# Attention matmuls of two sequences in one stretch, every second slot, and another order of the beginning

## The reference

```python
# layer 0: conditioned layer norm
out = (x - mean) * rsqrt(var + 1e-5) * weight + bias
out = (out + tanh(cond @ lin_w.T + lin_b)[:, None, :]) * weight + bias
# layer 1: conditioned transformer block, each gamma, beta, alpha = (cond @ w.T)[:, None, :]
h = gamma_a * rmsnorm(x) + beta_a
q, k, v = heads(h @ W_q.T), heads(h @ W_k.T), heads(h @ W_v.T)     # 16 heads of 16
x = x + alpha_a * (softmax(0.25 * q @ k.T) @ v) @ W_o.T            # per sequence, 64 x 64
h = gamma_f * rmsnorm(x) + beta_f
x = x + alpha_f * ((silu(h @ gate_w.T) * (h @ hidden_w.T)) @ out_w.T + out_b)   # 1024 hidden
```

## Time and profile before

| | |
|---|---|
| median of 3 runs | 1042.36 us (1040.92 to 1042.98) |
| the profiled execution | 1042.48 us, span 1040.7 us |
| busy TensorE / VectorE / ScalarE / GpSimd | 989.9 / 682.4 / 619.2 / 567.3 us |
| share of the span | 95 / 66 / 59 / 55 % |
| mean granted clock of TensorE | 0.988 of 2.4 GHz |
| first scores (L376) | 32.15 us |
| last small product of the attention (L398, slot 130) | 987.5 us |

### The profile page before, as it was taken

The page is one execution under the profiler, slowest core; times in us unless marked ns, Lnnn a source line. Parts: engine busy times, 40 slices in busy tenths (PEclk is TensorE's granted clock), DMA queues, the critical chain, the costliest instruction groups (busy, mean ns, idle before and its releaser), DMA issues.

```text
span 1040.7 us, 28677 instructions
## 1 busy us (share of the span) xinstructions
PE 989.9 (95%) x11292; PEld 920.9 (88%) x11292; DVE 682.4 (66%) x1310; ACT 619.2 (59%) x1733; POOL 567.3 (55%) x531
## 2 busy tenths in 40 slices
PE   5777999999999999999999999999999999999997
PEld 4665998999999999999999999999999899999897
DVE  4677666666666666676666667666676766666554
ACT  3456565666566566656656665665666566666432
POOL 3477646566474656647465564746656474443320
PEclk9889999999999999999999999999999999999999
DMA  6010001000100000000000000001000000000000
GB/s 203 2 62 21 2 11 33 11 23 12 32 12 12 32 12 22 12 30 15 12 32 12 22 12 17 27 12 32 12 22 12 12 13 12 12 12 13 11 12 21
DMA packets 20884, 23.37 MB, mean 22 GB/s; under 512 B 1168, under 2 KB 20240, under 8 KB 20752
## 3 DMA queue, kind: packets, MB, share of 16 engines
q1 hardware_dynamic: 20752, 21.54, 6.4%
HBM read 13.15 MB, written 8.39 MB: 21 GB/s over the span
## 4 chain that ended last, share of the span: by engine, by line
PE 68%; DVE 9%; ACT 7%; issue 7%; ACTq 0%; POOLq 0%; POOL 0%; DVEq 0%
PE psum L263 13%; PE psum L265 12%; PE psum L264 12%; PE psum L387 5%; PE psum L453 4%; PE psum L452 4%; PE psum L376 4%; PE psum L451 4%; PE psum L398 3%; ACT probs L778 3%; PE psum L293 1%; PE psum L301 1%; PE psum L306 1%; DVE merge L510 1%; DVE least L547 1%
## 5 line engine op out<-in xcount | busy, mean ns | idle before, releaser
L263 PE MATMUL psum<-xf_hi,ffn_hi 128*128 128x256 f32 x1024 | 287.6, 281 | 3.9 <-DVE normed_f L589 1.6
L264 PE MATMUL psum<-xf_lo,ffn_hi 128*128 128x256 f32 x1024 | 286.2, 280 | 0.0
L265 PE MATMUL psum<-xf_hi,ffn_lo 128*128 128x256 f32 x1024 | 285.6, 279 | 0.0
L778 ACT ACTIVATE probs<-psum,least 128x64 f32<-128x64 f32 x928 | 202.4, 330 | 50.1 <-DVE least L547 26.7
L612 DVE SCALAR_TENSOR_TENSOR late<-tanh,psum 128x512 f32<-128x512 f32 x128 | 88.1, 688 | 207.1 <-ACT tanh L801 206.8
L944 POOL TENSOR_TENSOR probs<-probs,inv_sum 128x512 f32<-128x512 f32 x128 | 141.9, 1109 | 128.3 <-DVE inv_sum L565 127.6
L807 ACT ACTIVATE prod_hi<-late 128x512 fp32r<-128x512 f32 x128 | 80.8, 631 | 210.4 <-DVE late L620 210.4
L263 PEld LDWEIGHTS psum<-xf_hi,ffn_hi 128*128 128x128 f32 x1024 | 192.5, 188 | 5.1 <-issue 3.8
L264 PEld LDWEIGHTS psum<-xf_lo,ffn_hi 128*128 128x128 f32 x1024 | 192.7, 188 | 0.0
L265 PEld LDWEIGHTS psum<-xf_hi,ffn_lo 128*128 128x128 f32 x1024 | 192.6, 188 | 0.0
L626 DVE TENSOR_TENSOR prod_lo<-late,prod_hi 128x512 fp32r<-128x512 f32 x128 | 88.7, 693 | 89.3 <-ACT prod_hi L807 89.3
(11 more groups left out here) (100 smaller groups left out, 2264.0 us busy)
## 6 DMA issues: line engine op xcount, KB each, us to landing
xin<-x_dram SPq DMA_DIRECT2D x16, 512.0 KB, 3.8
out_t_dram<-x_res SPq DMA_DIRECT2D x32, 256.0 KB, 2.1
w_raw<-attn_w_dram SPq DMA_DIRECT2D x1, 1024.0 KB, 7.6
x_res<-gate_w_dram SPq DMA_DIRECT2D x1, 1024.0 KB, 10.4
late<-hidden_w_dram SPq DMA_DIRECT2D x1, 1024.0 KB, 12.1
x_res<-out_w_dram SPq DMA_DIRECT2D x1, 1024.0 KB, 5.6
k_heads<-mod_w_dram SPq DMA_DIRECT2D x1, 448.0 KB, 5.4
ident<-identity_dram SPq DMA_DIRECT2D x1, 64.0 KB, 3.3
```

Source lines behind the costliest of these rows:

```text
L263: pe.matmul(out, stat_hi, mov_hi, start=first, stop=False)
L264: pe.matmul(out, stat_hi, mov_lo, start=False, stop=False)
L265: return pe.matmul(out, stat_lo, mov_hi, start=False, stop=last)
L778: op = act.activation(probs[g % 2][:, h * SEQ:(h + 1) * SEQ], scores[:, h // 2, h % 2], ACT.Exp, bias=least[g % 2][:, h:h + 1], scale=-1.0)
```

## The change

The slots of attention are paired. TensorE has nothing of attention in odd slots. In even slots it turns sequence s-2 (into bank 0, as before) and s-1 (into the last 128 columns of banks 3 to 6, `odd_turned`), multiplies s-4 and s-3 with the values, and makes the scores of s and s+1. VectorE finds both minima in the even slot, behind both scores. The exponentials, row sums and reciprocals of the odd sequence stay in the odd slot; GpSimd normalises both in the odd slot, the even one first and the odd one last. ScalarE copies both turned tiles in the even slot, the odd one only when both new minima are found. `centre` is left to even sequences. The mean-square matmuls (j = 1) go behind the projection. In odd slots `invert_sums` goes ahead of `activate`; the statistics of the tokens go behind `product`. In the beginning the loads have another order and are split in halves, weights of the FFN are split from slot -4 on, and queries and values of part 0 have another bank, so that keys, queries and norms follow each other in another order.

```diff
@@ constants
-SPLIT_AT = -1
+SPLITS = {-4: (0, 1), -3: (2,), -2: (3,), 0: (4,), 1: (5,), 2: (6,), 3: (7,), 4: (8,), 5: (9,), 6: (10,), 7: (11,)}
+OUT_W_AT = -1
@@ PSUM
-        scores = psum[:, 3:7, 0:2 * SEQ].rearrange("p r (a k) -> p r a k", k=SEQ)
-        attended_t = psum[:, 3:7, 2 * SEQ:4 * SEQ].rearrange("p s (h t) -> p h s t", h=2)
+        scores = [psum[:, 3:7, i * P:(i + 1) * P].rearrange("p r (a k) -> p r a k", k=SEQ) for i in range(2)]
+        attended_t = psum[:, 3:7, 2 * P:3 * P].rearrange("p s (h t) -> p h s t", h=2)
+        odd_turned = psum[:, 3:7, 3 * P:4 * P]
@@
         def wide(g):
-            return g < FFN_AT
+            return g < FFN_AT and g % 2 == 0
+        def norm_step(s):
+            return 3 if s == -2 else 2 if s == -1 else s % PSEQ
+        def proj_bank(w, m):
+            return y_bank if m == 0 and w in (WQ, WV) else work
@@ SyncE, loads
-            load_x(0)
+            sp.dma_start(cond_sb[0:COND, 0:BATCH], cond_t).then_inc(mod_loaded, 16)
+            load_mod(SHIFT, A_BETA, mod_loaded)
+            load_half(0)
             sp.dma_start(ident[:], identity).then_inc(loaded, 16)
...
-            sp.dma_start(cond_sb[0:COND, 0:BATCH], cond_t).then_inc(mod_loaded, 16)
-            sp.dma_start(mod_stage[:, 0:7 * D].rearrange("p (w d) -> p w d", d=D),
-                         mod_w.rearrange("w c d -> c w d")).then_inc(mod_loaded, 16)
+            load_half(1)
+            load_mod(A_BETA, F_ALPHA + 1, rest_loaded)
@@ TensorE
             def score_banks_free(s):
                 if is_seq(s - 1):
                     pe.wait_ge(scores_read, s)
-                if s % PSEQ == 3 and is_part(s // PSEQ - 1):
-                    pe.wait_ge(att_lo_made, s // PSEQ)
+                if is_seq(s - 3):
+                    pe.wait_ge(probsT_out, s - 2)
+                if s % PSEQ == 0 and is_part(s // PSEQ - 2):
+                    pe.wait_ge(att_lo_made, s // PSEQ - 1)
@@ turn_probs
                 pe.wait_ge(probs_made, g + 1)
-                if g >= 1:
-                    pe.wait_ge(probsT_out, g)
-                if g + 2 - FFN_AT >= 1:
+                if g % 2 == 0 and g + 2 - FFN_AT >= 1:
                     pe.wait_ge(act_made, g + 2 - FFN_AT)
@@ TensorE, the slot
-                if is_seq(s - 2):
-                    turn_probs(s - 2)
-                score_banks_free(s)
-                if is_seq(s - 3):
-                    times_values(s - 3)
-                if is_seq(s):
-                    score(s)
-                norm_bank_free(s)
+                if s % 2 == 0:
+                    if is_seq(s - 2):
+                        turn_probs(s - 2)
+                    score_banks_free(s)
+                    if is_seq(s - 1):
+                        turn_probs(s - 1)
+                    for g in (s - 4, s - 3):
+                        if is_seq(g):
+                            times_values(g)
+                    for g in (s, s + 1):
+                        if is_seq(g):
+                            score(g)
+                if norm_step(s) != 1 or s < 0:
+                    norm_bank_free(s)
...
+                if s == 0:
+                    values(0)
                 if j == 0 and is_part(grp + 1):
                     keys(grp + 1)
...
+                if norm_step(s) == 1 and is_group(grp) and s >= 0:
+                    norm_bank_free(s)
+                    mean_squares(grp)
                 if is_step(f):
                     gate(f)
@@ VectorE, the slot
-                if is_seq(s):
-                    find_least(s)
-                    if wide(s):
-                        centre(s)
+                if s % 2 == 0:
+                    for g in (s, s + 1):
+                        if is_seq(g):
+                            find_least(g)
+                            if wide(g):
+                                centre(g)
...
-                if grp % 2 == 0 and 2 <= (grp + 4) // 2 < NBLK:
-                    token_stats((grp + 4) // 2, j)
+                if s % 2 == 1 and is_seq(s):
+                    invert_sums(s)
                 if is_step(f):
                     activate(f)
-                if is_seq(s):
+                if s % 2 == 0 and is_seq(s):
                     invert_sums(s)
                 if is_step(f):
                     product(f)
...
+                if grp % 2 == 0 and 2 <= (grp + 4) // 2 < NBLK:
+                    token_stats((grp + 4) // 2, j)
+                    if j == 3:
+                        merge_stats((grp + 4) // 2, (grp + 4) // 2 + 2)
@@ ScalarE
+            def score_minima_found(g):
+                if is_seq(g + 1):
+                    act.wait_ge(least_made, g + 2)
+                    if wide(g) or wide(g + 1):
+                        act.wait_ge(scores_read, g + 1 + wide(g + 1))
@@ probs_out
+                if g % 2 == 1:
+                    score_minima_found(g + 1)
@@ ScalarE, the slot
-                if is_seq(s - 2):
+                if s % 2 == 0 and is_seq(s - 2):
                     probs_out(s - 2)
...  squares (j == 0) stand here
+                if s % 2 == 0 and is_seq(s - 1):
+                    probs_out(s - 1)
                 if j == 2 and is_part(grp - 1):
                     attended_hi(grp - 1)
@@ GpSimd, the slot
-                if is_seq(s - 1):
+                if s % 2 == 1 and is_seq(s - 1):
                     normalise_probs(s - 1)
...
                 if j == 1 and is_part(grp - 4):
                     add_ffn(grp - 4)
+                if s % 2 == 1 and is_seq(s):
+                    normalise_probs(s)
```

More of the change, by code:

```diff
@@ L226, in load_x, with load_half, load_mod @@
                              ).then_inc(x_loaded[b % 2], 16)
+            def load_half(i):
+                sp.dma_start(xin[0][:, 2 * i:2 * i + 2], x[i * PART:(i + 1) * PART, :].rearrange("(t p) d -> p t d", p=P)
+                             ).then_inc(half_loaded if i == 0 else x_loaded[0], 16)
+            def load_mod(first, last, signal):
+                sp.dma_start(mod_stage[:, first * D:last * D].rearrange("p (w d) -> p w d", d=D),
+                             mod_w[first:last].rearrange("w c d -> c w d")).then_inc(signal, 16)
             def store(m):
@@ L521, in normalise_tokens, with merge_stats @@
-            def normalise_tokens(b):
-                dve.wait_ge(rstd_made, b + 1)
-                for t in range(TILES):
+            def merge_stats(b, no, tiles=slice(0, TILES)):
+                even_mean, odd_mean = stats[:, tiles, 1], stats[:, tiles, 4]
+                dve.wait_ge(stats_made, no)
+                dve.tensor_tensor(merge[:, 0, tiles], even_mean, odd_mean, ALU.add)
+                dve.tensor_tensor(merge[:, 1, tiles], even_mean, odd_mean, ALU.subtract)
+                dve.tensor_tensor(merge[:, 2, tiles], stats[:, tiles, 2], stats[:, tiles, 5], ALU.add).then_inc(merged, 1)
+                dve.wait_ge(merged, 2 * no - 1)
+                dve.tensor_scalar(mean[b % 2][:, tiles], merge[:, 0, tiles], 0.5, None, ALU.mult)
+                dve.scalar_tensor_tensor(out=merge[:, 3, tiles], in0=merge[:, 1, tiles], scalar=0.25,
+                                         in1=merge[:, 1, tiles], op0=ALU.mult, op1=ALU.mult)
+                dve.tensor_scalar(merge[:, 4, tiles], merge[:, 2, tiles], 1.0 / D, LN_EPS, ALU.mult, ALU.add
+                                  ).then_inc(merged, 1)
+                dve.wait_ge(merged, 2 * no)
+                dve.tensor_tensor(rstd[b % 2][:, tiles], merge[:, 3, tiles], merge[:, 4, tiles], ALU.add
+                                  ).then_inc(var_made, 1)
@@ L524, in normalise_tokens, with half_stats, normalise_half @@
+            def half_stats(i):
+                dve.wait_ge(half_loaded if i == 0 else x_loaded[0], 16)
+                for t in (2 * i, 2 * i + 1):
+                    op = dve.bn_stats(stats[:, t], xin[0][:, t])
+                op.then_inc(stats_made, 1)
+                merge_stats(0, i + 1, slice(2 * i, 2 * i + 2))
+            def normalise_half(b, i, no):
+                dve.wait_ge(rstd_made, no)
+                for t in (2 * i, 2 * i + 1):
                     op = dve.tensor_scalar(xin[b][:, t], xin[b][:, t], mean[b][:, t:t + 1], rstd[b][:, t:t + 1],
@@ L558, in invert_sums @@
             def invert_sums(g):
-                dve.wait_ge(exp_made if wide(g) else scores_read, g + 1)
+                if wide(g):
+                    dve.wait_ge(exp_made, sum(wide(i) for i in range(g + 1)))
+                else:
+                    dve.wait_ge(scores_read, g + 1)
                 dve.tensor_reduce(row_sum[g % 2][:], probs[g % 2][:].rearrange("p (h k) -> p h k", k=SEQ), AX_X,
@@ L863, in _ @@
                     half_tanh(f)
+                if s == 0:
+                    values_out(0)
+                for c in SPLITS.get(s, ()):
+                    if s < 0:
+                        split_ffn_weights(c)
                 if j == 0 and is_part(grp + 1):
@@ L867, in _ @@
                     queries_out(grp + 1)
```

(7 more changed lines are left out.)

136 lines of the change are left out of this document (73 added, 63 removed).

## The result

The changed kernel takes 1110.32 us (median of 4, 1109.76 to 1111.81) against 1041.64 for the kernel before in the same job: a ratio of 1.066 [1.064, 1.069], 69 us slower. I had said 1081, in a range that ended at 1096. The profiled execution took 1109.76, its span is 1108.0.

| place | before | after | predicted |
|---|---|---|---|
| slot 12 | 94.02 | 120.92 | 102 |
| slot 16, first turn begins | 126.96 | 150.73 | 131.9 |
| a group of four slots, steady part | 30.49 | 32.01 | 31.86 |
| slot 120 | 921.11 | 985.27 | |
| slot 120's scores to the end | 119.6 | 122.7 | 1.5 less |

A forecast was written before the change was run, and what follows sets the result against it. TensorE, busy 989.9 us and steadily without holes, was taken as the bound. 1042.5 + 35.6 for 26 steady groups + 4.9 for the beginning - 1.5 for the last slots = 1081.5, stated as 1081; whole range 1030 to 1096.

The forecast's parts named there:

- the stretch: TensorE's small turn, value and score matmuls: a pair of sequences takes 2.18 us instead of 2.58.
- the change does not do what it says: Rival on TensorE's small matmuls: a pair still costs the full 2.58 us, 1089 us; chance 0.12 shared with a longer chain.
- the statistics: Token statistics moved behind the product: TensorE's waits for L612 go, 0.5 us a group.
- the steady chain: Steady groups: the odd sequence's chain over the other engines delays its turn; 1.37 us more a group, 35.6 over 26.
- a possible hold: VectorE's subtraction held by GpSimd's normalisation in slot 1 of every second group: 0.45 us each, 6 us, outside the sum.
- the beginning: Slots before 16: pairs of 11.2 to 12.4 us, slot 16 near 131.9; +4.9 us, between -5 and +15.
- the tail: The last slots lose the small stretches of some four pairs: -1.5 us, between -3 and +2.
- The odd chain is longer still: Rival: subtraction held, +6, and opening 8 us longer, 1095 us; chance 0.12 shared with no saving.
- all hidden: Rival: all waits stay hidden, groups of 29.07 us and an unchanged beginning, 1004 us; chance 0.08.
- chain shorter: Rival: chain 2 us a group shorter than laid out, groups of 29.9, beginning gains 5, 1022 us; chance 0.12.

The follow-up runs named there:

- e1: Kernel before with only the token statistics moved, behind the product instead of ahead of activate: 1031.17 us, 0.991 of the kernel before.
- e8: Changed kernel with old beginning to slot 11, no norm-bank wait in slot 3, odd normalisation first, other ScalarE, VectorE, GpSimd reorders: 1024.39 us, 0.984 of before.
- e2: Changed kernel without the norm bank's wait for VectorE's product in slot 3 of a group: 1106.15 us, 1.063 of the kernel before.
- e3: Changed kernel with GpSimd's normalisation of the odd sequence put ahead of its two additions: 1097.01 us, 1.054 of the kernel before.
- e9: Changed kernel with VectorE's odd row sums and GpSimd's odd normalisation moved ahead of other items, before slot 12 only: 1098.67 us, 1.057 of the kernel before.
- e6: Changed kernel with 16 unused matmuls ahead of even slots' second turn and odd slots' projection, slots 2 to 12: 1104.57 us, 1.061 of the kernel before.
- e14: Changed kernel with odd sums and normalisation moved ahead before slot 12, plus 16 unused matmuls ahead of odd slots' projections: 1100.86 us, 1.057 of the kernel before.
- e7: Changed kernel with VectorE's scaling for the FFN ahead of the low part of the attended values: 1132.04 us, 1.087 of the kernel before.
- e12: Changed kernel with VectorE's FFN scaling moved ahead and the norm bank's wait removed in slot 3: 1103.3 us, 1.059 of the kernel before.
- e13: Changed kernel with VectorE's FFN scaling moved ahead, plus 12 unused matmuls ahead of the norm bank's wait: 1112.18 us, 1.068 of the kernel before.

## Why the prediction came out as it did

**Right: the stretch.** 2.18 us for a pair, to the hundredth, so "the change does not do what it says" is out. **Right: the statistics.** 0.5 us a group (e1).

**Nearly right: the steady chain.** Groups were laid out at 31.60 without and 32.12 with the normalisation of tokens; measured are 31.92 and 32.16, in the mean 32.01, so +39.4 for +35.6. That the same pairs take 2.2 us less a group once the order around them is mended (e8, 29.77) bears the reading out: the pairing loses by the chain between the sequences of one pair. Left out was one wait. In slot 3 the norm bank's wait for VectorE's product now stands at the head of the slot, in front of attention_out, which therefore starts at 10.25 and not at 9.4. Without that wait alone the kernel gains only 4 us, 2 of them in the steady part (e2), because the wait ends nearly together with the odd chain; it was this second path that I had not laid out.

**Held as weighed, worth unknown: L675.** In the prediction I gave the subtraction (L626 then) a possible hold in slot 1 of every second group, and left it out of the sum. Its durations in two stretches (least, median, longest in ns), first of the kernel after, then before:

```profile
L675 DVE TENSOR_TENSOR prod_lo<-late,prod_hi x35: 689/693/1235, 423.2 to 696.3; 128x512 fp32r<-128x512 f32 x35
```

```profile
L626 DVE TENSOR_TENSOR prod_lo<-late,prod_hi x36: 691/692/694, 426.9 to 693.0; 128x512 fp32r<-128x512 f32 x36
```

One with nearly double the time, beside GpSimd's normalisation, begins at 513.60, in slot 1 of a group. Between 150 and 983 us 24 of 104 are held in this way, 1.18 to 1.24 us long: in every second group one in slot 1, as weighed, and one at the start of slot 2, which I had not seen; before, none of 111 is. The Trainium skill (SBUF — State Buffer, Who interferes with whom) says that a VectorE instruction with two SBUF inputs and a GpSimd instruction that reads SBUF shut each other out for a whole instruction; the trace agrees, with 1.23 and 0.69 us. No run here takes that meeting away by itself, so what share it has in the 4 us between 35.6 and 39.4 is open. It is hardly large: e3 has 38 held subtractions and groups of 31.61, e8 has 52 and is the fastest of all.

**Wrong: the beginning.** The step that failed reads: "From there a pair costs the chain above without gate and tanh: [...] 11.2 to 12.4 us, five of them 58", and with it "slot 16 starts near 131.9: +4.9, between -5 and +15". The five pairs up to slot 12 took 13.1, 15.9, 15.3, 15.7 and 15.9 us, 76 in all for 58, and the term is +24, 9 us outside its own bound. The list of that step counts the work of the two sequences and leaves out what stands between them on the two in-order queues: L635, which waits for TensorE, in front of the odd row sums, and an inverse root and a normalisation of tokens in front of the odd normalisation. The trace of before had all of these operations; I had laid the steady pair out item by item and priced the opening by a sum. Mended, that is 12 us (e9). The clock was left out as well: TensorE works in short pieces there, the granted clock is 0.66, and the part of the stretch that lies in the chain takes 3.1 us for 1.8. In the original order matmuls that keep the clock up bring slot 12 forward by 7 us and slot 16 by 4.5 (e6); with the order mended they bring 0.55 us at slot 12 and nothing in all (e14). With the order mended slot 12 is at 109, mine was 102. Its second turn still waits for GpSimd for 3.1 us there; what makes these 7 us stays open.

**Wrong in sign, small: the tail**, +3.1 for -1.5. No run looked at it, so its cause is open.

**The rivals.** "The odd chain is longer still" (1095), with an opening 8 us longer, is the nearest, and its opening was still 11 us short. The sides "all hidden" and "chain shorter" are out. But e8 shows that the second, with 29.9 a group and 1022 us, is what a better interleaving of the same pairs reaches.

## What to carry to other kernels

When a consumer is moved nearer to its producer, write down everything that then stands in front of each link on its in-order queue, waits at the head of a slot included, and do so for the beginning too, where other items stand there than in the steady part. If two paths end within some tenths of a microsecond, edit both before judging either: one alone gave 4 or 13 us here, both 24 (in the steady part 2, 10 and 19). And a wait removed from the bound engine isn't a gain by itself: look at where its idle time gathers next, and at the granted clock behind it.

## What the hardware showed that I had not expected

Two pauses of TensorE of 0.65 and 0.88 us in a pair leave the granted clock at 1.00 (2.4 GHz) in the steady part. Merged into one of 1.80 us they let it fall, though TensorE had worked without a hole for the 3.28 us in front of the one shown (532.0 to 535.28). It goes to 1.2 GHz for 3.4 us (0.72 and 0.85 in the two windows around it). This happens behind 16 of the 25 pauses in the steady part, which are all of 1.79 to 1.82 us; what sets the other nine apart, no run here shows. In the mean it costs 0.9 us a group, 22 us in all (e7). Halving the pause (e12, 0.97 us) or filling it with idle matmuls (e13) brings the clock back to 1.00 and the time with it.
